# Last slots as stationary operand, rest products four sequences at a time, and scatters ahead of gathers on POOL

## The reference

```python
capacity = max(1, int(Sz * CAP_FACTOR / E) + 1)          # 512 * 2 / 8 + 1 = 129 slots for each of 8 experts
scores_t = swapaxes(softmax(x @ router_w.T), 1, 2)
gate_vals, sel_idx = top_k(scores_t, capacity)            # each expert picks 129 tokens of each sequence
tokens = x[b_idx, sel_idx]
h = gelu(einsum('becd,edh->bech', tokens, w1) + b1)       # 128 -> 512
y = einsum('bech,ehd->becd', h, w2) + b2                  # 512 -> 128
out = zeros_like(x).at[b_idx, sel_idx].add(y * gate_vals)
```

## Time and profile before

| profiled execution | |
|---|---|
| its time | 752.71 us, of which the span is 751.0 us |
| PE / PEld busy | 82% / 49% |
| DVE / ACT / POOL busy | 69% / 50% / 52% |
| mixture of experts, from the first gather to the end of the last scatter | 232.94 to 436.56 us |

### The profile page before, as it was taken

How to read it: one execution, slowest core, us unless ns; L and a number is a source line. 1 busy time by engine, 2 the same in 40 slices (tenths; PEclk the granted TensorE clock), 3 DMA queues, 4 the chain that set the end, 5 groups by cost and what they waited for, 6 DMA issues and landing times.

```text
span 751.0 us, 14209 instructions
## 1 busy us (share of the span) xinstructions
PE 618.1 (82%) x4111; PEld 369.9 (49%) x4111; DVE 521.4 (69%) x1779; ACT 374.9 (50%) x800; POOL 391.2 (52%) x529
## 2 busy tenths in 40 slices
PE   2478888888405999999799778999999999999894
PEld 1235555554302688776566533545454545444453
DVE  8458888887794112225478859898989898987554
ACT  0322333331450423326622357777777777767873
POOL 0077777776004777776887554343434343433341
PEclk9989999999855999999999989999999999999997
DMA  9400000000040122244663244040304030200011
GB/s 297 133 0 1 1 0 0 0 1 0 16 140 28 49 43 39 39 93 84 110 98 35 26 82 53 10 59 10 59 10 60 9 60 9 60 5 2 24 52 42
DMA packets 45145, 34.55 MB, mean 46 GB/s; under 512 B 4304, under 2 KB 41728, under 8 KB 45072
## 3 DMA queue, kind: packets, MB, share of 16 engines
q1 hardware_dynamic: 33584, 25.15, 14.5%
q0 software_dynamic: 10144, 7.90, 7.5%
q10 hardware_dynamic: 1344, 0.62, 0.3%
HBM read 14.13 MB, written 9.70 MB: 32 GB/s over the span
## 4 chain that ended last, share of the span: by engine, by line
PE 46%; DVE 16%; issue 8%; ACT 4%; POOL 1%; DMA 1%; DVEq 0%; ACTq 0%; POOLq 0%
PE bank L2146 8%; PE wide L1275 6%; DVE masked L1744 6%; PE wide L2133 5%; PE wide L2082 5%; PE wide L1283 4%; PE bank L1283 4%; PE bank L2082 2%; PE wide L2158 2%; ACT L282 1%; DVE mx L1744 1%; DVE slot_t L886 1%; POOL x_row L1045 1%; PE bank L2057 1%; PE bank L1300 1%
## 5 line engine op out<-in xcount | busy, mean ns | idle before, releaser
L1941 ACT ACTIVATE pexp<-wide 128x512 f32<-128x512 f32 (+2 forms) x384 | 180.9, 536 | 77.9 <-PE wide L2133 75.9
L1744 DVE CUSTOM_DVE_ANT_0 masked<-wide,mask_qk 128x128 f32<-128x128 f32 (+3 forms) x423 | 182.8, 477 | 46.9 <-PE wide L2082 46.1
L1872 POOL TENSOR_SCALAR_AFFINE_SELECT pexp<-pexp 128x256 f32<-128x256 f32 x256 | 106.4, 429 | 166.7 <-ACT pexp L1941 165.2
L2133 PE MATMUL wide<-qT,kTe 128*128 128x256 bf16 (+3 forms) x512 | 121.8, 301 | 6.1 <-ACT pexp L1941 3.7
L2082 PE MATMUL wide<-kTm,qT 128*128 128x128 bf16 (+3 forms) x423 | 102.6, 300 | 13.2 <-DVE mx L1744 10.8
L1036 POOL DMA_INDIRECT x_dram<-yg,row_u x56 | 89.4, 1597 | 30.6 <-DVE yg L1088 15.7
L1225 ACT ACTIVATE hT<-wide,b1T 128x512 f32<-128x512 f32 x64 | 43.9, 686 | 100.7 <-PE wide L1275 100.7
L1045 POOL DMA_INDIRECT x_row<-xln_dram,row_u x64 | 62.6, 978 | 52.5 <-DVE slot_tok L915 33.6
L2146 PE MATMUL bank<-pexp,vx 128*32 128x512 f32 (+3 forms) x1024 | 85.4, 446 | 4.9 <-POOL pexp L1872 4.9
L2133 PEld LDWEIGHTS wide<-qT,kTe 128*128 128x128 bf16 x512 | 48.6, 99 | 42.5 <-ACT pexp L1941 23.1
L1275 PE MATMUL wide<-xgT,w_sb 128*128 128x512 f32 x128 | 67.4, 612 | 1.5 <-ACT xgT L1218 1.5
(11 more groups left out here) (282 smaller groups left out, 1046.6 us busy)
## 6 DMA issues: line engine op xcount, KB each, us to landing
qT<-qp SPq DMA_DIRECT2D x126, 64.0 KB
x_sb<-in_L_attn_x SPq DMA_DIRECT2D x8, 256.0 KB, 6.7
w_sb<-in_L_ffn_w SPq DMA_DIRECT2D x1, 2048.0 KB, 13.1
xln_dram<-hT SPq DMA_DIRECT2D x8, 256.0 KB, 2.3
x_dram<-x_sb SPq DMA_DIRECT2D x7, 256.0 KB, 2.7
x_sb<-x_dram SPq DMA_DIRECT2D x7, 256.0 KB, 3.1
out_x<-x_sb SPq DMA_DIRECT2D x7, 256.0 KB, 2.3
qT<-qp_first SPq DMA_DIRECT2D x18, 64.0 KB
```

What stands on the lines that cost most here:

```text
L1744: ins = nc.vector.tensor_tensor_reduce(out=masked[:, n % 4, at], in0=bank_of(n)[:, at], in1=mask_qk[:, T - w:T], scale=1.0, scalar=LEAST, ...
L1872: nc.gpsimd.affine_select(out=pexp[:, at, :, 0:P], in_=pexp[:, at, :, 0:P], pattern=[[0, 2], [1, P]], compare_op=ALU.is_ge, fill=0.0, base ...
L1941: nc.scalar.activation(pexp[:, exp_slot(b, 2 * step + h // 2), h % 2:h % 2 + nh, 0:w], scores_bank(b, m)[:, 0:nh * w].rearrange("p (h t) - ...
L2133: ins = nc.tensor.matmul(scores_bank(b, m)[:, hh * w:(hh + 1) * w], kTe[:, par, j * P:(j + 1) * P], qT[:, b % QB, 4 * qd + h + hh, j * P:T ...
```

## The change

1. **Last slots.** The roles are swapped: the token columns, padded with zeros to 32 for each expert, are the stationary side, and w1 streams 512 columns against them; four experts write four groups of 32 partitions of one bank (8 products in phase 2 instead of 32). The rows are copied to `masked`, transposed by 8 PE transposes in phase 3, and b1 is added there. In phase 4 the 8 columns of each expert are stationary and w2 streams 128 columns (32 products, again in four partition groups). Two banks are now used. The rows come to their 64 partitions by 8 small DMAs of SP instead of a transpose.
2. **Rest.** All 8 sequences at once for each quarter of the tokens: two products of 32 rows and 512 columns, one for FIRST and one for SECOND, 8 products in phase 6 instead of 32 in phases 6 and 7. Sequence 0's rest is added by DVE.
3. **POOL.** For phases 4 to 11 the scatters of p come ahead of the gathers of p+4.

```diff
-        LAST_AT = {1: LAST_XT, 2: LAST_HIDDEN, 4: LAST_OUTPUT, 5: LAST_T}
+        LAST_AT = {1: LAST_XT, 2: LAST_HIDDEN, 3: LAST_HT, 4: LAST_OUTPUT, 5: LAST_ROWS}
+        REST_P, LAST_FILLS = 6, 4
@@ moe_sync
+            sp.wait_ge(m_taken, LAST_FILLS)
+            for g in range(G):
+                for j in range(E // G):
+                    sp.dma_start(y_last[j * G + g:BE:E, :], yl_rows[32 * g:32 * g + B, j * D:(j + 1) * D]).then_inc(m_yr, 16)
+            sp.wait_ge(m_taken, LAST_FILLS + NT)
             for b in DMA_SECOND:
-                sp.wait_ge(m_taken, fill_no["rest", b])
                 x_to_dram(sp, b, 1)
@@ moe_pool
+        SCATTERS_LEAD = 4
             for p in range(PHASES):
-                if p + 4 < PHASES:
+                if p < SCATTERS_LEAD:
                     pool_moe_gathers(pool, p + 4)
                 pool.wait_ge(m_y, p + 1)
                 ...
                         pool_moe_scatter(pool, p % E, b)
+                if SCATTERS_LEAD <= p < PHASES - 4:
+                    pool_moe_gathers(pool, p + 4)
@@ dve_moe_fold_rest, act_moe_keep_rest
+            dve.wait_ge(m_full, LAST_FILLS + k + 1)
+            nc.vector.tensor_tensor(x_sb[:, G:B, k, :], x_sb[:, G:B, k, :], side[1][:, :].rearrange("p (b d) -> p b d", d=D),
                                     ALU.add).then_inc(m_taken, 1)
+            act.wait_ge(m_full, LAST_FILLS + k + 1)
+            nc.scalar.activation(masked[:, k, :], side[0][:, :], ACT.Copy).then_inc(m_kept, 1)
@@ pe_moe_rest, pe_moe_last
+        def pe_moe_rest(pe, k):
+            pe.wait_ge(r_last.sem, r_last.total(1))
+            pe.wait_ge(m_rr, 1)
+            pe.wait_ge(m_taken, LAST_FILLS + k)
+            pe.wait_ge(m_kept, k)
+            for half in range(2):
+                rows = slice(32 * half, 32 * half + 32)
+                ins = nc.tensor.matmul(side[half][:, :], rest_l[rows, k * P:(k + 1) * P],
+                                       rest_r[rows, G * half:G * half + G, :].rearrange("r b d -> r (b d)"),
+                                       start=True, stop=True)
+            ins.then_inc(m_full, 1)
...
             elif stage_no == LAST_HIDDEN:
-                for e in two:
-                    for c in range(HC):
-                        at = (e * HC + c) * B
-                        ins = nc.tensor.matmul(side[:, at:at + B], w1_sb[:, e, c * P:(c + 1) * P],
-                                               xlT[:, :].rearrange("p (b e) -> p e b", e=E)[:, e, :], start=True, stop=True)
+                for g in range(G):
+                    ins = nc.tensor.matmul(side[j][32 * g:32 * g + 32, :], xlT[:, j * G + g, :], w1_sb[:, j * G + g, :],
+                                           start=True, stop=True)
+            elif stage_no == LAST_HT:
+                for c in range(HC):
+                    ins = nc.tensor.transpose(side[j][:, c * P:(c + 1) * P], h_last[:, j, c * P:(c + 1) * P], ident)
+            else:
                 pe.wait_ge(m_lh, 1)
+                for c in range(HC):
+                    for g in range(G):
+                        e = j * G + g
+                        ins = nc.tensor.matmul(side[0][32 * g:32 * g + B, j * D:(j + 1) * D], hl[:, e, c, :], w2_sb[:, e, c, :],
                                                start=c == 0, stop=c == HC - 1)
```

More of the change, by code:

```diff
@@ L812, in build @@
         new_stage()
+        FIRST, SECOND = tuple(range(G)), tuple(range(G, B))
+        BY_PE, DMA_FIRST, DMA_SECOND = FIRST[:1], FIRST[1:], SECOND
+        BY_DMA = DMA_FIRST + DMA_SECOND
+        SEQ = FIRST + SECOND
         rmax = scratch("rmax", [P, B * NT])
@@ L843, in build @@
         tokens_f = scratch("tokens_f", [P, T])
-        place = scratch("place", [P, 2, T])
+        place = scratch("place", [P, len(BY_PE), T])
         qp_first = scratch("qp_first", [P, PARTS, T], BF16)
@@ L1005, in placed_no @@
             return len(BY_PE) * e + BY_PE.index(b) + 1
-        LAST_XT, LAST_HIDDEN, LAST_OUTPUT, LAST_T = range(4)
-        LAST_AT = {1: LAST_XT, 2: LAST_HIDDEN, 4: LAST_OUTPUT, 5: LAST_T}
[L1011 to L1014, removed]
+        LAST_XT, LAST_HIDDEN, LAST_HT, LAST_OUTPUT, LAST_ROWS = range(5)
+        LAST_AT = {1: LAST_XT, 2: LAST_HIDDEN, 3: LAST_HT, 4: LAST_OUTPUT, 5: LAST_ROWS}
+        REST_P, LAST_FILLS = 6, 4
         def x_to_dram(sp, b, half):
@@ new lines, in dve_moe_last @@
+                nc.vector.tensor_copy(h_last[:, 1, :], side[1][:, :]).then_inc(m_taken, 1)
+            elif stage_no == LAST_HT:
+                for j in range(E // G):
+                    ins = nc.vector.tensor_tensor(
+                        hl_in[:, j * G:(j + 1) * G, :, :].rearrange("p g c b -> p c g b"),
+                        side[j][:, :].rearrange("p (c g r) -> p c g r", g=G, r=32)[:, :, :, 0:B],
+                        b1T[:, j * G * HC:(j + 1) * G * HC].rearrange("p (g c) -> p c g", c=HC).unsqueeze(3)
+                        .broadcast_to([P, HC, G, B]), ALU.add)
+                ins.then_inc(m_taken, 1)
+            elif stage_no == LAST_OUTPUT:
+                for g in range(G):
+                    rows = slice(32 * g, 32 * g + B)
+                    ins = nc.vector.tensor_tensor(yl_rows[rows, :].rearrange("b (j d) -> b j d", d=D),
+                                                  side[0][rows, 0:E // G * D].rearrange("b (j d) -> b j d", d=D),
+                                                  b2rep[rows, g::G, :], ALU.add)
+                ins.then_inc(m_taken, 1)
+            else:
+                dve.wait_ge(m_yr, 16 * E)
+                nc.vector.tensor_tensor(rest_r[0:BE, :, :], y_last.unsqueeze(1).broadcast_to([BE, B, D]),
+                                        by_seq, ALU.mult).then_inc(m_rr, 1)
@@ L1181, in moe_dve @@
                     dve_moe_last(dve, LAST_AT[p])
-                for i in range(1, G):
-                    if (p, i) in REST_AT and REST_AT[p, i] in DMA_SECOND:
-                        dve_moe_fold_rest(dve, REST_AT[p, i])
+                if p == REST_P:
+                    for k in range(NT):
+                        dve_moe_fold_rest(dve, k)
+                if p == REST_P + 1:
+                    dve_moe_first_rest(dve)
                 dve_moe_gated(dve, p)
@@ L1228, in act_moe_aside @@
         def act_moe_aside(act, p, i):
-            if p in LAST_AT and LAST_AT[p] == LAST_HIDDEN and i == G - 1:
-                act.wait_ge(m_taken, fill_no["last", LAST_HIDDEN])
+            if p in LAST_AT and LAST_AT[p] == LAST_HT and i == G - 1:
+                act.wait_ge(m_taken, LAST_HT + 1)
                 nc.scalar.activation(hl[:, :, :, :], hl_in[:, :, :, :], ACT.Gelu).then_inc(m_lh, 1)
-            if (p, i) in REST_AT and REST_AT[p, i] in DMA_FIRST:
-                act_moe_keep_rest(act, REST_AT[p, i])
+            if p == REST_P:
+                act_moe_keep_rest(act, i)
             if (p, i) in XT_AT_P:
@@ L1320, in pe_moe_last @@
                 pe.wait_ge(m_lh, 1)
-                for e in two:
-                    for c in range(HC):
-                        ins = nc.tensor.matmul(side[:, e * B:(e + 1) * B], w2_sb[:, e, c, :], hl[:, e, c, :],
+                for c in range(HC):
+                    for g in range(G):
+                        e = j * G + g
+                        ins = nc.tensor.matmul(side[0][32 * g:32 * g + B, j * D:(j + 1) * D], hl[:, e, c, :], w2_sb[:, e, c, :],
                                                start=c == 0, stop=c == HC - 1)
-            elif stage_no == LAST_T and i == G - 1:
-                ins = nc.tensor.transpose(side[0:BE, 0:D], ylT[:, :, :].rearrange("p b e -> p (b e)"), ident)
@@ L1332, in pe_moe_side @@
                 pe_moe_scatter(pe, p - 1, BY_PE[i - 1])
[L1333 to L1342, removed]
+            if p in LAST_AT and LAST_AT[p] < LAST_ROWS and i in (1, 2):
+                pe_moe_last(pe, LAST_AT[p], i - 1)
+            if p == REST_P:
+                pe_moe_rest(pe, i)
             if (p, i) in XT_AT_P:
                 if XT_AT_P[p, i] == 0:
-                    pe.wait_ge(m_taken, len(fill_no))
+                    pe.wait_ge(m_taken, LAST_FILLS + NT)
+                    pe.wait_ge(m_kept, NT)
                 pe_xT(pe, XT_AT_P[p, i], first=True)
```

63 lines of the change are left out of this document (29 added, 34 removed).

## The result

The changed kernel takes 769.61 us (median of 4 runs, 768.97 to 771.06) against 752.55 us before (4 runs, 749.36 to 752.98): ratio 1.0239, 95% interval 1.0207 to 1.0270, slower by 17 us. The profiled execution took 771.06 us (span 769.3), 18.35 more than that of before. The forecast was 764.9 us and a range of 754 to 774: the direction and the mechanism came out, the size was 5 us too small.

What follows compares the result with a forecast made beforehand. PE bounds the kernel, with POOL close behind; gating, scatters, gathers and landing would outlast a phase and stop PE. The chain puts t(13) 12.1 us later, added to the profiled 752.71: 764.9 us, range 754 to 774.

Steps and rivals of the forecast that it cites:

- The margin of 5.5 us: Before the change, phase 13's gathers land at 368.6 and PE wants them at 374.13.
- t(8): Start of PE's transposes in phase 8 (t(p) likewise for phase p): forecast 339.1, before 340.56.
- t(13): Start of PE's transposes in phase 13: forecast 409.5, before 397.31; nothing waits for gathers from there on.
- The sign of 3 to 5 us of idle time in almost every phase: Sign of being right: PE's transposes idle that long before them, released by gathers, from phase 6 on.
- Part 1: Last slots: phase 2 saves 5.16 us, phase 3 gains about 1.0, phase 4 loses 7.15 and gains 3.6.
- Part 2: Rest: phases 6 and 7 fall from 26.93 to 22.3 us; pairs at 1.06 each, new wait 1.4.
- the 12.3 of the forecast: Fall of PE's work in phases 2 to 7, in us, from last slots and rest.
- The clock charge: 1.5 us for PE's lower clock behind each of the stops at t(6), t(8) and t(10).
- Landing under load: With four scatters, the last gather lands 4.4 us after its start, 16.3 after the first scatter.
- Hidden gathers: Rival: gathers do not hold PE and its 12.3 us carry to the end, 740.4 us; chance 0.12.
- No overlap: Rival: new small products run one after another, phases 2, 4, 6 longer by 4.9, 3.5, 3.4; 776.7 us; chance 0.10.
- the mild stop: Rival: landings of 2.5 us, no clock loss, outputs at 1.8, no wait at second pair; 756.8 us; chance 0.23.

Runs made afterwards that it cites:

- e1: Changed kernel with POOL's old order in all phases (gathers of p+4 ahead of scatters of p), last slots and rest kept: 746.65 us, ratio to before 0.991.
- e2: Kernel before, with only POOL's order changed (scatters ahead of gathers in phases 4 to 11): 774.58 us, ratio 1.0282.
- e6: Changed kernel with scatters first from phase 4, but five token buffers instead of four, gathers issued five phases ahead: 749.58 us, ratio 0.9964.
- e5: Changed kernel with gathers first in all phases, as in e1, and DVE's list reordered in phases 6 and 9: 743.0 us, ratio 0.9882.
- e4: Changed kernel with idle products of 512 columns ahead of the transposes in phases 6, 8, 10 and 12, keeping PE busy: 762.34 us, ratio 1.014.
- e7: The kernel of e1 run once more, on the chip of e5: 745.14 us, ratio 0.9907.
- e8: Changed kernel with scatters first and five token buffers, as in e6, and DVE's list reordered as in e5: 750.19 us, ratio 0.9978.
- e3: Changed kernel with scatters first only in phases 8 to 11, not from phase 4: 757.63 us, ratio 1.0073.

## Why the prediction was right, and where it was off

**Bound and turning point: right.** The margin of 5.5 us was not enough for four scatters and four gathers. PE stops from phase 6 on, t(8) came at 342.04 (forecast 339.1), t(13) at 414.52 (409.5). The sign of 3 to 5 us of idle time in almost every phase came only in part: the steps let gathers set t(11) and t(13) too, where the trace has no stop, and the stops at t(10) and t(12) are longer instead, 6.83 and 6.66. At t(13) the 17.2 us lie above the 8 to 14 of the text. e1 and e2 separate the two parts, and e6 shows the loop itself.

**Part 1: right, at the lower end.** Phase 2 takes 10.72 (10.3 forecast), phase 3 9.22 (9.3). Two groups at 1.0 were taken, and 0.99 is what each takes. For 8 stationary columns twice the lower end was taken; 16 products take 0.99 us, close to the lower end, and phase 4 takes 10.71 instead of 12.0. Nothing came of these 1.3 us. The forecast has the scatters of 4 wait for their gating; they found POOL still at the scatters of 3 [0.30 <-issue], so POOL's own list set t(6) at 310.14, close to the 310.5 of the text.

**Part 2: the mechanism right, the pair priced a little too low.** The new wait is 1.37 us (1.4 forecast). The halves of a pair overlap: they start at 323.06 and 323.07 us. The Trainium skill says that products in different row groups run at the same time ("TensorE: Matmul & The Clock Gate", Packing small matmuls). The trace agrees, with these two starts. In e5, which has neither the wait nor a low clock, phase 6 takes 13.35 us from its transposes to those of phase 7:

```profile
304.92 0.60 PE L1295 MATMUL wide<-cst,x_row 128*128 128x128 f32 x4
...
318.27 0.60 PE L1295 MATMUL wide<-cst,x_row 128*128 128x128 f32 x4
```

Less the plain 8.34 that is 5.01 for four pairs, 1.25 each and not 1.06: the pair 1.05, and the group ahead of it and the group behind it 0.1 longer each. The Trainium skill has a rule that a change of tiling mode drains the engine ("TensorEngine Tiling (Array Packing)", Key Properties). The trace agrees so far, with products of L1307's kind at 1.16 behind a pair and 1.05 in a plain phase. In e6, where no gather holds phases 2 to 7, these take 62.13 us against 74.68 before: the 12.5 us saved are the 12.3 of the forecast.

**The clock charge: mis-sized.** 1.5 us were charged behind each of three stops, from one group that took 3.21 instead of 1.71. That row shows the price of one group, not how long the state lasts. Phase 6 without clock loss, with the wait, takes 14.80 us (e6); after the stop of 5.73 it took 18.84, so the clock cost 4.0 there. Over all stops e4 puts it at 7.3 us or more, where 4.5 stood in the sum; the stop of 6.66 at t(12) had no charge at all.

**Landing under load: mis-sized at two places.** 4.4 us were taken from the earlier trace rows for each landing from phase 8 on. From the start of the last gather to PE's transposes are 370.51 - 364.52 = 6.0 us for phase 12's tokens and 402.26 - 394.76 = 7.5 for phase 14's. The median landing from 340 to 395 us is 4.1 us, no longer than before, but PE waits for the last of four, and the earlier trace rows already has landings of up to 6.3. In these two stretches the DMA engines' mean share (the number before the last) is 0.70 and 0.69; other transfers, in the first of them q's rows by SP, move with the gathers. That these make the landing longer fits, but no run tests it:

```profile
364.50:370.50 6.00, 0.00 (x0) 0.00 (x0) 1.18 (x8) 1.29 (x3) 5.06 (x4) 0.67 0.70 110
394.80:402.20 7.40, 0.80 (x2) 0.00 (x0) 2.23 (x10) 0.69 (x1) 6.62 (x5) 0.90 0.69 86
```

**The sum.** Against the forecast's steps, from t(2) on: phases 2 and 3 together 0.3 long, phase 4 1.3 short and phase 5 1.2 long, phases 6 and 7 3.3 long (2.5 of it clock), phase 8 0.6, phase 9 0.8, phase 10 1.1 short, phase 11 3.7 long (3.1 of it landing), phase 12 1.8 short. Together 5.6. As t(2) came 0.6 earlier than before, t(13) is 5.0 later than forecast, and from there to the end of the span it is 1.1 us longer than before: 6.2 over the forecast for the profiled execution. The median lies 4.7 over it. The direction rests on the loop as forecast; that the miss stayed this small is partly luck, as errors of 4.2 us in phases 4, 10 and 12 stand against 9.8 in the others.

**The rivals.** Hidden gathers: no, but e1 is nearly that world, and there 746 and not 740.4 us come out. That number let all of PE's 12.3 us arrive at the end; with POOL's list full from 250 to 400 us, at most 9 of them did (e5). No overlap: excluded by the rows above. Of the mild stop only the cheap outputs came (phase 4 at 10.71); the landings of 6.0 and 7.5 us, the clock of 0.50 and the wait of 1.37 speak against it.

## What to carry to other kernels

Before two steps of a queue change places, write down the loop that runs through them (here gating, scatters, gathers, landing, transposes, gating) and compare its length with the time that the buffers give it; one buffer more (e6) was worth 20 us where the order itself was worth none. A stop of PE costs its length and then the slow clock behind it, so take that from a whole stage and not from one group. And after shortening the full engine, look for the list that has no pauses left: it can set what arrives.

## What the runs showed of the hardware that was not expected

Behind a short wait the granted clock fell in some executions and not in others. Phase 6 with POOL's gathers in time has only the wait of 1.37 us at the second pair, in e6 and e7 alike. The windows of 4 us that follow it, in e6 and then in e7:

```profile
313.03:317.03 4.00, 4.00 (x19) 1.73 (x20) 0.69 (x1) 1.29 (x3) 3.08 (x4) 1.00 0.16 44
```
```profile
312.73:316.73 4.00, 4.00 (x8) 0.99 (x8) 0.08 (x1) 0.77 (x2) 3.18 (x3) 0.50 0.25 40
316.73:320.73 4.00, 4.00 (x14) 2.31 (x14) 0.61 (x1) 1.20 (x2) 3.39 (x3) 0.66 0.44 40
```

The phase takes 14.80 us in e6 and 18.05 in e7, nearly as much as behind the stop of 5.73 us in the changed kernel (18.84); without the wait it takes 13.35 (e5, and e8 too). With the same wait e3 has 14.79 at a clock of 1.00, and e1 16.43 with a stretch at 0.61. So a wait of 1.4 us in a dense stretch came to between 1.4 and 4.7 us. No kernel here was made to find what decides between the two.
